# Two row scatters in flight in a fused attention and mixture-of-experts kernel

## The chip, the core and the metric

The kernel runs on one core of one Trainium2 chip. The metric is the device time of one execution in microseconds (us), the median of several runs.

## What is computed

The input is `x`, 8 sequences of 512 tokens with 256 channels (4096 tokens), in float32. One layer is computed: `x + attention(layernorm(x)) + ffn(layernorm(x))`. The attention takes a second-order Taylor series in place of the exponential. The part that matters here is the mixture of experts:

```python
logits = xf @ Wg
top_w, top_i = jax.lax.top_k(logits, TOP_K)
top_w = jax.nn.softmax(top_w, axis=-1)
one_hot = jax.nn.one_hot(top_i, E, dtype=xf.dtype)
combine = jnp.einsum('nk,nke->ne', top_w, one_hot)
h = jnp.einsum('nc,ech->enh', xf, W1)
g = jnp.einsum('nc,ech->enh', xf, W2)
y = jnp.einsum('enh,ehc->enc', jax.nn.silu(h) * g, W3)
out = jnp.einsum('enc,ne->nc', y, combine)
```

There are 8 experts (E), each token uses 2 of them (TOP_K), and an expert has 512 hidden channels. The output of a token is so the sum of its attention row and of two weighed expert rows.

## The kernel before, in words

The program is written by hand for each engine, with semaphores between the engines. It has two halves.

The first half runs over 8 batches of 512 tokens: layer norm, attention, the gate logits and the routing. GpSimd scatters each normed row twice into a scratch in HBM (`xs_scr`), sorted by expert (L467). The attention's output rows, with x added, are stored to `out` by SyncE's queue.

The second half is the mixture of experts. It runs over NT = 71 tiles of 128 sorted rows. Since each expert's rows are rounded up to whole tiles, the number of tiles in use depends on the data; 71 is the most there can be, and the rest are spare tiles, which read zero rows and add them to 128 rows behind the output. For a tile t:

- GpSimd gathers 128 rows into `xg`, four tiles ahead (`gather`, L485), and adds the 128 finished rows of the tile to `out` in HBM with an accumulating scatter (`scatter`, L496). In GpSimd's program `gather(t + 4)` stands ahead of `scatter(t)`.
- TensorE transposes the rows (L1171), multiplies with W1 and W2 (`up`, L1182), transposes the hidden rows (L1191) and multiplies with W3 (`down`, L1203). Every product is made of three, from high and low parts of float32.
- ScalarE rounds to the high parts (L619, L625), and makes the high parts of the weights of the first tiles on the way (`w12_high` L576, `w3_high` L580). VectorE makes the low parts (`expert_x` L979, `low_s` L988, `w12_low` L706, `w3_low` L711), multiplies the two hidden halves (L1009), and weighs the output rows into `yo` (`weigh_y`, L996), which has two buffers. For the first tiles TensorE waits for those low parts of the weights.
- SyncE's queue loads the weights; the last ones are issued after attention's buffers are free.

An accumulating scatter reads a row, adds and writes it. Two tiles of one expert name different tokens, but a tile of the next expert can name the same token again, and all spare tiles name the same 128 rows. Before the change each scatter waits until the one before it has landed, by one count:

```python
                    e.wait_ge(s["d_sc"], 16 * t)
```

VectorE's helper `then` lets every small instruction of the routing wait for its own semaphore before the next one starts, so these run one by one. `experts()` (L873 to L875) makes the table of each tile's expert, `texp`, which TensorE and VectorE read into a register for each tile (L1208, L991); its semaphore `v_te` also tells SyncE's queue that attention's last constants are read, so that W3 of experts 6 and 7 may be loaded over them (L396 to L398).

Of the kernel before, what the change touches and what calls it, by code (L numbers as in the profile page):

```python
# [10 lines left out]
NE = 8  # L11
HID = 512
H = 16
NT = 2 * NB + NE - 1
# [18 lines left out]
I32 = mybir.dt.int32  # L33
U32 = mybir.dt.uint32
ALU = mybir.AluOpType
# [77 lines left out]
def build(nc, x, wqk, wv, wo, w12, w3, out):  # L113
    with ExitStack() as ctx:
        s = {}
# [32 lines left out]
        minus = keep.take("minus", 4)  # L148
        A0 = room - 49152
        B0, D0, E0 = A0 + 8192, A0 + 16384, A0 + 32768  # L150
        W3h = Region(A0, B0).take("w3h", 8192, F32R, (NE * 4, D))
# [6 lines left out]

        rm = Region(344, A0)
        xg = rm.take("xg", GR * XW, F32, (GR, XW))  # L160
# [7 lines left out]

        rq = Region(344, A0)
        K2 = rq.take("K2", 2048, F32R, (2, 2, 512))  # L170
# [27 lines left out]
        def w12_lo(n):  # L198
# [76 lines left out]
                "v_rt", "v_M", "p_rk", "v_d", "a_ex", "v_slots", "v_te", "v_cw", "v_li", "p_gl", *(f"d_g{i}" for i in range(GR)), "p_gt", "a_gt", "v_gt", "v_xw", "p_h", "p_g",  # L275
                "a_si", "v_mu", "p_st", "a_st", "v_st", "p_yo", "v_yo", "d_sc")
        MISC, USED = misc_uses()
# [45 lines left out]
        def sync_program(e):  # L323
# [71 lines left out]
            done(e, "G", 0, 0)  # L395
            e.wait_ge(s["v_te"], 1)  # L396
            for n in range(6, 8):
# [4 lines left out]
            load_w12(15)  # L402
            e.wait_ge(s["d_sc"], 16 * NT)


        def gpsimd_program(e):
# [21 lines left out]
            for j in range(4):  # L428
                e.memset(below[:, j, j:4], 1.0).then_inc(s["c_below"], 1)
            e.wait_ge(s["c_iota"], 1)  # L430
            e.tensor_copy(iota[:], iota_i[:]).then_inc(s["c_const"], 1)
# [12 lines left out]
            for u in range(2):  # L444
                e.memset(xb[u][:, :, D + NE:XW], 0.0).then_inc(s["c_const"], 1)
            e.memset(zero[:], 0.0).then_inc(s["c_z"], 1)
            e.wait_ge(s["c_z"], 1)
            e.iota(zero[:, D + NE:D + NE + 1].bitcast(I32), pattern=[[0, 1]], base=NTOK, channel_multiplier=1).then_inc(s["c_z"], 1)
# [39 lines left out]
            def scatter(t):  # L488
                e.wait_ge(s["v_yo"], t + 1)
                if t == 0:  # L490
                    for b in range(4, NBATCH):
                        out_sent(e, b)
                    e.wait_ge(s["d_z"], 32)
                else:
                    e.wait_ge(s["d_sc"], 16 * t)
                e.indirect_dma_start(out, bass.IndirectOffsetOnAxis(xw[:, t % 4, NE:NE + 1].bitcast(U32), 0), yo[:, t % 2, :], None,  # L496
                                     compute_op=ALU.add).then_inc(s["d_sc"], 16)

# [157 lines left out]
        def vector_program(e):  # L656
            count = {"v_rt": 0, "v_M": 0, "v_d": 0, "v_slots": 0, "v_te": 0, "v_cw": 0, "v_li": 0,
                     "v_nt": 0}
# [214 lines left out]
            def experts():  # L873
                then(e.tensor_reduce(tf[:], cmp[:], AX.X, ALU.add))
                then(e.tensor_copy(texp[:], tf[:]), "v_te")  # L875

            e.memset(banks[:, 4, :], 0.0).then_inc(s["c_b4"], 1)
            e.wait_ge(s["c_p"], 1)
# [98 lines left out]
            def expert_x(t):  # L977
# [4 lines left out]
                if t >= 4:  # L982
                    e.wait_ge(s["d_sc"], 16 * (t - 3))
                e.tensor_copy(xw[:, t % 4, :], xg[:, t % GR, D:XW]).then_inc(s["v_xw"], 1)
# [5 lines left out]
            def weigh_y(t):  # L990
# [3 lines left out]
                if t >= 2:  # L994
                    e.wait_ge(s["d_sc"], 16 * (t - 1))
                e.tensor_scalar(yo[:, t % 2, :], banks[:, 6 + t % 2, 0:256], xw[:, t % 4, bass.ds(expert, 1)], None,  # L996
# [6 lines left out]
            for t in range(NT + 1):  # L1003
# [8 lines left out]
                if t == 0:  # L1012
                    step("o", LAST, 1)
                    w3_low(0)
                if t + 1 < NE:
                    w3_low(t + 1)
# [262 lines left out]
```

## Time and profile before

| | |
|---|---|
| median of 3 runs | 668.18 us (668.07 to 668.24) |
| span of the profiled execution | 665.4 us |
| TensorE busy | 641.8 us, 96% of the span |
| VectorE busy | 410.6 us, 62% |
| ScalarE busy | 341.6 us, 51% |
| GpSimd busy | 344.1 us, 52% |
| scatters to `out` (L496) | 71, 112.2 us busy, 154.4 us idle ahead of them |
| granted TensorE clock, mean | 0.996 |

The profile gives the span of its execution, from the first to the last instruction; no other time of that execution is recorded, and the median of the runs is 2.8 us more than the span. Busy time counts the work of an engine and not its waits for semaphores, its register loads or the issue of a DMA. What GpSimd is busy with at L485 and L496 is the making of the transfer's descriptors; the transfer itself lands later. In the names PE is TensorE, DVE VectorE, ACT ScalarE, POOL GpSimd and SP SyncE; a q behind the name is the engine's sequencer.

### The profile page before, as it was taken

How to read it: one execution, taken by the hardware profiler on the slowest of the kernel's cores; microseconds unless marked ns; L12 is line 12 of the kernel's file. 1: busy time of each engine (PE TensorE's matmuls, PEld its weight loads, DVE VectorE, ACT ScalarE, POOL GpSimd, SP SyncE). 2: the span in 40 equal slices, each digit the busy share in tenths (PEclk: the TensorE clock that was granted, in tenths of full speed). 3: DMA queues.
4: the chain of work that ended last, by engine and by line, in shares of the span. 5: the costliest groups of instructions: out<-in, count | busy, mean ns of one | idle time of the engine just before them, and what ended most of it. 6: DMA issues, size and time to landing. Idle time of an engine off the chain costs nothing.

```text
span 665.4 us, 16423 instructions
## 1 busy us (share of the span) xinstructions
PE 641.8 (96%) x5414; PEld 496.5 (75%) x5414; DVE 410.6 (62%) x1067; ACT 341.6 (51%) x515; POOL 344.1 (52%) x381
## 2 busy tenths in 40 slices
PE   8899999999999999999999999999999999999994
PEld 7555666666666666657888888888888888888883
DVE  6777788787878585777975444444544445444452
ACT  3668878787877686766642232322323223232331
POOL 3265655546463736473465555455545555455542
PEclk9999999999999999999999999999999999999998
DMA  4653555554443435447633434333333433333332
GB/s 134 141 133 99 127 153 130 152 130 147 93 136 77 128 85 154 118 150 249 207 59 58 66 51 66 50 57 60 58 59 50 66 51 57 58 51 58 58 50 25
DMA packets 37775, 64.07 MB, mean 96 GB/s; under 512 B 8289, under 2 KB 25825, under 8 KB 37697
## 3 DMA queue, kind: packets, MB, share of 16 engines
q0 software_dynamic: 16704, 28.12, 22.0%
q1 hardware_dynamic: 20432, 34.24, 20.2%
q8 instruction: 50, 0.82, 0.5%
q10 hardware_dynamic: 560, 0.66, 0.3%
q14 instruction: 29, 0.23, 0.1%
HBM read 27.72 MB, written 22.68 MB: 76 GB/s over the span
## 4 chain that ended last, share of the span: by engine, by line
PE 87%; DVE 4%; DMA 2%; ACT 2%; issue 2%; SPq 1%; ACTq 0%; POOL 0%; POOLq 0%; DVEq 0%
PE banks L1182 29%; PE banks L1203 15%; PE banks L1056 10%; PE banks L1038 8%; PE banks L1076 7%; PE banks L1191 5%; PE banks L1085 4%; PE banks L1120 3%; PE banks L1171 2%; PE banks L1105 1%; PE banks L1111 1%; DMA K<-Kt 1%; ACT T L533 1%; DVE xTl L740 1%; PE banks L1094 1%
## 5 line engine op out<-in xcount | busy, mean ns | idle before, releaser
L496 POOL DMA_INDIRECT out<-yo,xw x71 | 112.2, 1581 | 154.4 <-DVE yo L996 76.6
L625 ACT ACTIVATE sTh<-banks 128x512 fp32r<-128x512 f32 x71 | 42.5, 598 | 192.4 <-PE banks L1191 186.6
L476 POOL TENSOR_SCALAR_AFFINE_SELECT T<-T 128x512 f32<-128x512 f32 x128 | 80.8, 642 | 108.5 <-ACT T L539 43.1
L988 DVE TENSOR_TENSOR sTl<-banks,sTh 128x512 fp32r<-128x512 f32 x71 | 49.0, 691 | 118.9 <-ACT sTh L625 118.9
L1182 PE MATMUL banks<-w12h,xgh 128*128 x284 | 118.0, 415 | 0.6 <-DVE xgl L979 0.6
L1182 PE MATMUL banks<-w12l,xgh 128*128 x284 | 112.2, 395 | 0.0
L1182 PE MATMUL banks<-w12h,xgl 128*128 x284 | 112.1, 395 | 0.0
L485 POOL DMA_INDIRECT xg<-xs_scr,glist x71 | 72.4, 1020 | 21.5 <-issue 20.0
L1056 PE MATMUL banks<-T,vau 128*17 128x512 f32 (+3 forms) x1024 | 75.6, 434 | 0.9 <-POOL T L476 0.9
L467 POOL DMA_INDIRECT xs_scr<-xb,slots x64 | 64.3, 1004 | 18.7 <-issue 10.0
L1038 PE MATMUL banks<-Q,K 32*128 32x256 f32 (+2 forms) x1024 | 70.5, 358 | 3.5 <-DMA K<-Kt 2.2
L525 ACT ACTIVATE T<-banks 128x1024 f32<-128x1024 f32 x64 | 62.1, 1026 | 12.5 <-PE banks L1038 11.9
L533 ACT ACTIVATE T<-banks 128x768 f32<-128x768 f32 x64 | 48.5, 810 | 27.2 <-PE banks L1038 27.2
L1182 PEld LDWEIGHTS banks<-w12h,xgl 128*128 128x128 f32 x284 | 53.3, 188 | 12.0
L1056 PEld LDWEIGHTS banks<-T,vau 128*17 128x17 f32 x1024 | 26.0, 97 | 46.3 <-issue 38.4
L1182 PEld LDWEIGHTS banks<-w12h,xgh 128*128 128x128 f32 x284 | 53.8, 189 | 7.8 <-issue 1.0
L1038 PEld LDWEIGHTS banks<-Q,K 32*128 32x128 f32 x1024 | 38.6, 183 | 27.1 <-ACT T L525 12.7
L1182 PEld LDWEIGHTS banks<-w12l,xgh 128*128 128x128 f32 x284 | 53.9, 190 | 6.3
L996 DVE TENSOR_SCALAR yo<-banks,xw 128x256 f32<-128x256 f32 x71 | 34.3, 483 | 39.0 <-PE banks L1203 31.2
L539 ACT ACTIVATE T<-banks 128x768 f32<-128x768 f32 x64 | 48.7, 810 | 18.0 <-PE banks L1038 16.1
L1009 DVE TENSOR_TENSOR hs<-banks,hs 128x512 f32<-128x512 f32 x71 | 49.1, 692 | 10.2 <-PE banks L1182 0.9
L1203 PE MATMUL banks<-w3h,sTh 128*128 x284 | 51.1, 302 | 0.8 <-ACT sTh L625 0.8
(174 smaller groups left out, 1222.3 us busy)
## 6 DMA issues: line engine op xcount, KB each, us to landing
Q<-Q SPq DMA_DIRECT2D x128, 64.0 KB, 2.4
w12r<-w SPq DMA_DIRECT2D x16, 512.0 KB, 4.2
out<-xa SPq DMA_DIRECT2D x16, 256.0 KB
w3r<-w SPq DMA_DIRECT2D x8, 512.0 KB, 8.7
K<-Kt SPq DMA_DIRECT2D x124, 32.0 KB
xa<-x SPq DMA_DIRECT2D x7, 512.0 KB, 4.7
xg<-xs_scr,glist POOLq DMA_INDIRECT x71
out<-yo,xw POOLq DMA_INDIRECT x71
```

The source lines that it names most:

```text
L467: e.indirect_dma_start(xs_d, bass.IndirectOffsetOnAxis(slots[:, k, 4 * b + blk:4 * b + blk + 1].bitcast(U32), 0), xb[b % 2][:, blk, :], No ...
L476: e.affine_select(out=v, in_=v, pattern=[[0, 4], [1, P]], compare_op=ALU.is_ge, fill=-1.0, base=0, channel_multiplier=-1).then_inc(s["g_mk ...
L485: e.indirect_dma_start(xg[:, t % GR, :], None, xs_d, bass.IndirectOffsetOnAxis(glist[:, t:t + 1].bitcast(U32), 0)).then_inc(s[f"d_g{t % GR ...
L496: e.indirect_dma_start(out, bass.IndirectOffsetOnAxis(xw[:, t % 4, NE:NE + 1].bitcast(U32), 0), yo[:, t % 2, :], None, compute_op=ALU.add) ...
L525: e.activation(T0[n % 2][:, 2 * h:2 * h + 2, :], banks[:, 2 * h:2 * h + 2, :], ACT.Square, scale=0.25, bias=1.0).then_inc(s["a_s"], 1)
L533: e.activation(T1[:, 2 * h:2 * h + 2, :], banks[:, 2 * h:2 * h + 2, 0:384], ACT.Square, scale=0.25, bias=1.0).then_inc(s["a_s"], 1)
L988: e.tensor_tensor(sTl[:], banks[:, 5, :], sTh[:].bitcast(F32), ALU.subtract).then_inc(s["v_st"], 1)
L1009: e.tensor_tensor(hs[:], banks[:, 2 * (t % 2) + 1, :], hs[:], ALU.mult).then_inc(s["v_mu"], 1)
L1038: i = e.matmul(banks[:, r, c0:c0 + w], K2[rr, g, h, jm * P:(jm + 1) * P], Q2[g][rr, h, p, 512 - w:512], start=(p == 0), stop=(p == 1))
L1056: i = e.matmul(banks[32 * r:32 * r + HA, 4, 512 - w:512], vau[b % 2][:, jm, 4 * qd + r, :], v[:, r, :], start=(jm == 0), stop=(jm == 2), s ...
L1182: i = e.matmul(banks[:, 2 * (t % 2) + m, :], a[:, k, :], w[:, bass.ds(expert[t] * 4 + (2 * k + m), 1), :], start=(k == 0 and n == 0), stop ...
L1203: i = e.matmul(banks[:, 6 + t % 2, 0:256], a[:, k * P:(k + 1) * P], w[:, bass.ds(expert[t] * 4 + k, 1), :], start=(k == 0 and n == 0), sto ...
```

## The change

A scatter no longer waits for the one before it in every tile, but always for the one before that, on two semaphores `d_sc0` and `d_sc1` for even and odd tiles. Whether it also waits for the one just before is read from a table `held`: for scatter t the entry t - 1 is 16 * ((t - 1) // 2), plus 16 where tile t belongs to another expert than tile t - 1 or is a spare tile. GpSimd makes a constant `before` at the start, VectorE makes `held` in four instructions (`holds`) right after `w3_low(0)` in tile 0, and GpSimd reads an entry into a register before each scatter from t = 3 on. An instruction on four elements (`mark`) carries the wait for that register, and `g_hold` counts it. SyncE's loads of W3 for experts 6 and 7 wait for `v_hold` in place of `v_te`. The scratch for the descriptors of GpSimd's transfers is 8192 bytes per partition; the new tiles take some of the room.

```diff
@@ sync_program
-            e.wait_ge(s["v_te"], 1)
+            e.wait_ge(s["v_hold"], 1)
             for n in range(6, 8):
                 load_w3(n)
...
-            e.wait_ge(s["d_sc"], 16 * NT)
+            for u in range(2):
+                e.wait_ge(s[f"d_sc{u}"], 16 * ((NT + 1 - u) // 2))
@@ gpsimd_program
+            e.iota(before_i[:], pattern=[[16, 36], [0, 2]], base=0, channel_multiplier=0).then_inc(s["c_hold"], 1)
             e.wait_ge(s["c_iota"], 1)
             e.tensor_copy(iota[:], iota_i[:]).then_inc(s["c_const"], 1)
...
             e.memset(zero[:], 0.0).then_inc(s["c_z"], 1)
+            e.wait_ge(s["c_hold"], 1)
+            e.tensor_copy(before[:], before_i[:]).then_inc(s["c_hold"], 1)
@@ scatter(t)
-                else:
-                    e.wait_ge(s["d_sc"], 16 * t)
+                if t >= 3:
+                    if t == 3:
+                        e.wait_ge(s["v_hold"], 1)
+                    else:
+                        e.wait_ge(s["g_hold"], t - 3)
+                    count = 16 * ((t - 1) // 2)
+                    landed = e.value_load(held[0:1, t - 1:t], min_val=count, max_val=count + 16)
+                    e.wait_ge(s[f"d_sc{(t - 1) % 2}"], landed)
+                    e.tensor_tensor(mark[:], minus[:], minus[:], ALU.add).then_inc(s["g_hold"], 1)
+                    e.wait_ge(s[f"d_sc{t % 2}"], 16 * (t // 2))
+                elif t:
+                    e.wait_ge(s[f"d_sc{(t - 1) % 2}"], 16)
                 e.indirect_dma_start(out, bass.IndirectOffsetOnAxis(xw[:, t % 4, NE:NE + 1].bitcast(U32), 0), yo[:, t % 2, :], None,
-                                     compute_op=ALU.add).then_inc(s["d_sc"], 16)
+                                     compute_op=ALU.add).then_inc(s[f"d_sc{t % 2}"], 16)
@@ vector_program
+            def holds():
+
+                e.wait_ge(s["c_hold"], 2)
+                then(e.tensor_scalar(change[:], iota[:, 0:72], end[:, NE - 1:NE], None, ALU.is_ge))
+                then(e.tensor_tensor(part[:, 0:71], tf[:, 1:72], tf[:, 0:71], ALU.subtract))
+                then(e.tensor_tensor(change[:, 1:72], change[:, 1:72], part[:, 0:71], ALU.max))
+                then(e.scalar_tensor_tensor(held[:, 0:71], change[:, 1:72], 16.0, before[:, 0:71], ALU.mult, ALU.add), "v_hold")
...
                 if t >= 4:
-                    e.wait_ge(s["d_sc"], 16 * (t - 3))
+                    e.wait_ge(s[f"d_sc{t % 2}"], 16 * (t // 2 - 1))
...
                 if t >= 2:
-                    e.wait_ge(s["d_sc"], 16 * (t - 1))
+                    e.wait_ge(s[f"d_sc{t % 2}"], 16 * (t // 2))
...
                 if t == 0:
                     step("o", LAST, 1)
                     w3_low(0)
+                    holds()
                 if t + 1 < NE:
                     w3_low(t + 1)
@@ kernel
-    nc = bacc.Bacc("TRN2", target_bir_lowering=False, num_devices=1)
+    nc = bacc.Bacc("TRN2", target_bir_lowering=False, num_devices=1, dynamic_dma_scratch_size=8192)
```

On VectorE, at the start of the second half (the rest of tile 0 and the start of tile 1), there stood before (w3l and w12l are low parts of weights, sTl and xgl those of the hidden and of the gathered rows):

```order
L779 TENSOR_TENSOR xa_129<-banks,xa_129 128x512
L711 TENSOR_TENSOR w3l<-w3r,w3h 128x1024 x2
L706 TENSOR_TENSOR w12l<-w12r,w12h 128x1024
L988 TENSOR_TENSOR sTl<-banks,sTh 128x512
L1009 TENSOR_TENSOR hs<-banks,hs 128x512
L979 TENSOR_TENSOR xgl<-banks,xgh 128x256
```

and in the changed kernel (whose line numbers are 23 to 31 higher here):

```order
L802 TENSOR_TENSOR xa_134<-banks,xa_134 128x512
L734 TENSOR_TENSOR w3l<-w3r,w3h 128x1024
L903 TENSOR_SCALAR change<-iota,end 128x72
L904 TENSOR_TENSOR part<-tf 128x71
L905 TENSOR_TENSOR change<-change,part 128x71
L906 SCALAR_TENSOR_TENSOR held<-change,before 128x71
L734 TENSOR_TENSOR w3l<-w3r,w3h 128x1024
L729 TENSOR_TENSOR w12l<-w12r,w12h 128x1024
L1019 TENSOR_TENSOR sTl<-banks,sTh 128x512
L1040 TENSOR_TENSOR hs<-banks,hs 128x512
L1010 TENSOR_TENSOR xgl<-banks,xgh 128x256
```

Four instructions have come between the low parts of W3 of experts 0 and 1. On GpSimd, at the end of the program, there stood before (the last two gathers and the scatters of tiles 65 to 70, the last five of them in one row):

```order
L485 DMA xg<-xs_scr,glist 128x272
L496 DMA out<-yo,xw 4224x256
L485 DMA xg<-xs_scr,glist 128x272
L496 DMA out<-yo,xw 4224x256 x5
L1239 UNCONDITIONAL_BRANCH
```

and in the changed kernel (the scatters of tiles 68 to 70):

```order
L519 DMA out<-yo,xw 4224x256
L513 TENSOR_LOAD held
L513 ISA x2
L515 TENSOR_TENSOR mark<-minus 128x4
L519 DMA out<-yo,xw 4224x256
L513 TENSOR_LOAD held
L513 ISA x2
L515 TENSOR_TENSOR mark<-minus 128x4
L519 DMA out<-yo,xw 4224x256
L1271 UNCONDITIONAL_BRANCH
```

Ahead of each scatter from tile 3 on there is now a register load with two instructions of the sequencer and one small computing instruction.

## Rows read from the trace of the kernel before

**Rows 1.** busy time of each engine in three stretches (us, then instructions), granted clock, DMA

```profile
309.00:320.00 11.00, 10.25 (x62) 8.61 (x61) 9.83 (x15) 7.28 (x11) 0.00 (x0) 1.00 1.02 377
320.00:650.00 330.00, 330.00 (x2031) 287.79 (x2030) 165.27 (x349) 107.73 (x212) 175.16 (x134) 1.00 0.36 60
```

**Rows 2.** waits between 320 and 650 us: total, times, longest

```profile
POOL out L496 <- DVE yo L996: 70.2, 35, 3.3
POOL out L496 <- DMA out<-yo,xw: 47.4, 26, 3.2
...
DVE yo L996 <- DMA out<-yo,xw: 7.0, 12, 0.6
```

**Rows 3.** timeline of one steady tile, GpSimd: start, duration, instruction, idle before it

```profile
483.99 1.58 POOL L496 DMA_INDIRECT out<-yo,xw  x1 [1.99 <-DVE yo L996]
485.88 0.99 POOL L485 DMA_INDIRECT xg<-xs_scr,glist  x1 [0.30 <-issue]
```

**Rows 4.** chain that ended last, 309 to 318 us: start, duration

```profile
311.06 0.69 DVE xa L779
311.75 2.27 DVE w3l L711 x2
314.01 0.28 DVE w12l L706
...
316.35 0.34 DVE xgl L979
...
316.89 1.19 PE banks L1182 x4
```

**Rows 5.** timeline of the last tiles, weighed rows and their scatters

```profile
650.05 1.55 POOL L496 DMA_INDIRECT out<-yo,xw  x1 [3.30 <-DVE yo L996]
...
653.93 0.48 DVE L996 TENSOR_SCALAR yo<-banks,xw 128x256 f32<-128x256 f32 x1 [0.77 <-DMA out<-yo,xw]
...
654.69 1.55 POOL L496 DMA_INDIRECT out<-yo,xw  x1 [3.09 <-DVE yo L996]
...
656.90 0.48 DVE L996 TENSOR_SCALAR yo<-banks,xw 128x256 f32<-128x256 f32 x1 [1.32 <-PE banks L1203]
659.25 1.55 POOL L496 DMA_INDIRECT out<-yo,xw  x1 [3.00 <-DMA out<-yo,xw]
```

**Rows 6.** chain that ended last, one piece at its end

```profile
654.69 3.80 DMA out<-yo,xw
```

**Rows 7.** timeline of short VectorE instructions, each waiting for the one before

```profile
281.46 0.22 DVE L837 TENSOR_SCALAR rk<-end,pf 128x8 f32<-128x8 f32 x1
...
284.72 0.23 DVE L851 TENSOR_TENSOR sel<-step,rk 128x64 f32<-128x64 f32 x1
284.99 0.22 DVE L852 TENSOR_REDUCE gapt<-sel 128x8 f32<-128x64 f32 x1
...
293.00 0.34 DVE L864 SCALAR_TENSOR_TENSOR lists<-rown,gapt,dummy 128x128 f32<-128x128 f32 x1
```

**Rows 8.** VectorE's register loads: minimum, median, longest ns, then first and last start

```profile
L991 DVEq TENSOR_LOAD <-texp x71: 299/304/590, 316.8 to 654.9; - x71
...
L991 DVEq SEQ_ASSERT  x71: 23/23/35, 317.6 to 655.5; - x71
```

**Rows 9.** GpSimd's groups of small instructions: busy us, mean ns

```profile
L411 POOL TENSOR_TENSOR sm<-sm,minus 128x4 f32<-128x4 f32 x8 | 8.4, 1048 | 12.6 <-DVE sm L680 12.4
L456 POOL COPY xb<-ids_i 128x4 int32<-128x4 int32 x8 | 1.5, 192 | 0.0
```

**Rows 10.** timeline of GpSimd, a row transfer behind a computing instruction

```profile
75.14 0.98 POOL L467 DMA_INDIRECT xs_scr<-xb,slots  x1 [0.17 <-issue]
```

**Rows 11.** waits of the whole span, GpSimd for VectorE's variances

```profile
POOL sm L411 <- DVE sm L680: 12.4, 2, 9.9
```

**Rows 12.** timeline of the DMA issues of SyncE

```profile
312.27 0.92 SPq L339 DMA_DIRECT2D w3r<-w  x2
```

**Rows 13.** timeline of ScalarE, the rounding of W3 for expert 6

```profile
335.54 1.05 ACT L580 ACTIVATE w3h<-w3r 128x1024 fp32r<-128x1024 f32 x1
```

More of the change, by code:

```diff
@@ L149, in build @@
         A0 = room - 49152
+        Q1 = 4056
         B0, D0, E0 = A0 + 8192, A0 + 16384, A0 + 32768
@@ L157, in build @@
         banks = ctx.enter_context(nc.psum_tensor("banks", [P, 8, 512], F32))
-        rm = Region(344, A0)
+        rm = Region(344, Q1)
         xg = rm.take("xg", GR * XW, F32, (GR, XW))
@@ L167, in build @@
         xw = rm.take("xw", 64, F32, (4, 16))
-        rq = Region(344, A0)
+        rx = Region(Q1, A0)
+        held = rx.take("held", 72, I32)
+        mark = rx.take("mark", 4)
+        before_i = rx.take("before_i", 72, I32)
+        before = rx.take("before", 72)
+        change = rx.take("change", 72)
+        rq = Region(344, Q1)
         K2 = rq.take("K2", 2048, F32R, (2, 2, 512))
@@ L275, in build @@
                 "v_rt", "v_M", "p_rk", "v_d", "a_ex", "v_slots", "v_te", "v_cw", "v_li", "p_gl", *(f"d_g{i}" for i in range(GR)), "p_gt", "a_gt", "v_gt", "v_xw", "p_h", "p_g",
-                "a_si", "v_mu", "p_st", "a_st", "v_st", "p_yo", "v_yo", "d_sc")
+                "a_si", "v_mu", "p_st", "a_st", "v_st", "p_yo", "v_yo", "d_sc0", "d_sc1",
+                "c_hold", "v_hold", "g_hold")
         MISC, USED = misc_uses()
@@ L656, in vector_program @@
         def vector_program(e):
-            count = {"v_rt": 0, "v_M": 0, "v_d": 0, "v_slots": 0, "v_te": 0, "v_cw": 0, "v_li": 0,
+            count = {"v_rt": 0, "v_M": 0, "v_d": 0, "v_slots": 0, "v_te": 0, "v_cw": 0, "v_li": 0, "v_hold": 0,
                      "v_nt": 0}
```

## Prediction

> **What bounds the kernel now.** I read first the busy time by stretches, then who waits for whom, then the chain of work that ended last at the two places where it leaves TensorE. From 320 to 650 us, the mixture of experts once its weights are ready, TensorE is busy for 330.00 of 330.00 us [rows 1]. A tile has 30 of its instructions (12 with W1 and W2, 12 with W3, 6 transposes), so 2031 of them in 330 us are 67.7 tiles, 4.87 us each. The waits that the change is about are in the same stretch: the scatter waits 47.4 us in all for the one before it, in 26 of the tiles, and VectorE's weighing of the rows waits 7.0 us for a scatter, at most 0.6 us at once [rows 2]. None of it reaches TensorE. A steady tile on GpSimd shows why: 1.58 us for the scatter, 0.30, 0.99 for the gather, then 1.99 us with nothing to do but wait for the next weighed rows [rows 3]. So where the old wait stands in most tiles, it costs nothing.
>
> At two places something else than TensorE sets the end. In the first, 309 to 320 us, TensorE stands still for 11.00 - 10.25 = 0.75 us, and VectorE is busy for 9.83 [rows 1]. The chain goes there through VectorE from 311.06 to 316.69 us: the last attention rows, two low parts of W3, one of W1 and W2, the low and the hidden rows, `xgl`, and only then TensorE's `up` of tile 2 at 316.89 [rows 4]. The second is the end: the last two scatters. Tile 69's rows are ready at 653.93 + 0.48 = 654.41, its scatter starts at 654.69 (0.28 later), and tile 70's rows have been ready since 657.38 when its scatter starts at 659.25 behind a wait for a transfer [rows 5]. The chain has that transfer as a piece of 3.80 us, from 654.69 to 658.49 [rows 6]; the last scatter starts 0.76 us after it.
>
> **The four instructions of `holds`.** They stand between the two low parts of W3, in the middle of VectorE's part of the chain, and each waits for the one before. Instructions of this kind take 0.22 us with 8 elements and a scalar from a tensor, 0.23 with 64 and 0.34 with 128 and three inputs, and the next starts 284.99 - 284.72 - 0.23 = 0.04 us after the end [rows 7]. For 71 or 72 elements I take 0.28, 0.23, 0.23 and 0.25, with 4 x 0.04: 1.15 us. Bounds: four at 0.22, 1.04 with the gaps; four at 0.34, 1.52. What is queued behind them on VectorE is all that the chain goes through, and TensorE is at that time already waiting for it, so the 1.15 us pass on in full. Afterwards TensorE has no slack in which to win them back. Term: **+1.15 us**.
>
> **The register load and the mark.** Before each scatter from tile 3 on, GpSimd's sequencer, once the weighed rows are there, loads the register, checks it, waits for the landing with `mark`, runs `mark`, and then starts the scatter. From the start of such a load on VectorE to the end of its check pass 655.5 + 0.02 - 654.9 = 0.6 us, of which the load is 0.30 (median; 0.59 the longest) [rows 8]. A GpSimd instruction on 128x4 takes 0.19 us as a copy, 1.05 as the power in `root` [rows 9]; an addition is nearer to the copy, and I take 0.2. A transfer behind a computing instruction starts 0.17 us after it [rows 10]. That makes 0.6 + 0.2 + 0.17 = 0.97 us per scatter. In the steady tiles GpSimd's 1.99 us of waiting hide it [rows 3], and 1.0 us is left; behind it are queued the gathers, which run four tiles ahead. If that cover were gone, each tile would cost up to 0.97 us, 66 us in all.
>
> At the end there is no cover. Tile 69's scatter starts 0.97 us later, and its landing too; the one before it, which started at 650.05 [rows 5] and takes 3.80 [rows 6], has landed in either kernel. For tile 70 the load is over before the landing, and what is new behind the landing is `mark` and the gap: 0.37 us. Does tile 70 still wait for tile 69? The reference's seeded inputs, routed by its own formula, give the experts 1057, 1055, 981, 1014, 1007, 1010, 1022 and 1046 rows, that is 9 + 9 + 8 + 8 + 8 + 8 + 8 + 9 = 67 tiles. Tiles 67 to 70 are spare ones, and the table asks for the wait in each. So nothing is saved there. Term: **+1.34 us**. Bounds: 0.8 + 0.3 = 1.1 with a short check; with a load of 0.59 and `mark` like the power, 0.29 + 0.6 + 1.05 + 0.17 and 1.05 + 0.17, together 3.3 us.
>
> The row says 0.30 us for a register load, and the Trainium skill ("DMA: Bandwidth & Descriptors", Latency and other measured facts) gives a floor of some 600 ns for `tensor_load`. No median here agrees with that, only the longest one does. By the page the sum would be 0.3 us more.
>
> **What costs nothing.** The two constants on GpSimd, 0.2 us each, are made while it waits for VectorE's variances, 12.4 us in two waits of which one is 9.9 [rows 11]. SyncE's loads of W3 for experts 6 and 7 were issued at 312.27 us [rows 12]; behind `holds` they come at about 314, and the first of them is needed at 335.54 [rows 13]. The wait of `yo` and `xw` for a scatter is for the same tile as before. For the smaller descriptor scratch no row shows a price: all scatters take 1.55 to 1.58 us [rows 3, 5]. I take 0, and it would show as longer scatters or gathers.
>
> **The sum.** 1.15 + 1.34 = 2.49 us on the profiled span of 665.4, so 667.9 us of span. The runs are 2.8 us above the span, and the same difference on the other side gives 668.18 + 2.49 = **670.7 us**, 0.37% slower. Two versions of this kernel can be told apart at about 0.2%, 1.3 us.
>
> **Rivals.**
> - *One of the two costs is covered.* VectorE's order could leave a hole, so that `holds` costs nothing at TensorE. For it speaks that VectorE is busy for only 9.83 of those 11.00 us [rows 1]; against it, that the chain's pieces on VectorE follow each other without a hole from 311.06 us on [rows 4]. Then 668.18 + 1.34 = 669.5 us, on the edge of what can be told. Chance 0.10.
> - *The last scatter is freed* (the side of no change). If tile 70 were not held, its scatter would start at 657.38 + 0.28 + 0.97 = 658.63 and not at 659.25, 0.62 us earlier than before, and the time would be 668.18 + 1.15 - 0.62 = 668.7 us. It turns on one number, the entry 69 of the table, so on whether all 71 tiles are in use; the count of 67 speaks against it. Chance 0.05.
> - *GpSimd becomes the bound.* Its loop would be 0.28 + 0.6 + mark + 0.17 + 1.58 + 0.30 + 0.99 us, 4.12 with a mark of 0.2. From a mark of 0.95 on it is longer than the tile's 4.87, and the power's 1.05 is beyond that [rows 9]. The gathers ahead would hide most of the lag, and the end would pay the dear marks: 668.18 + 1.15 + 3.04 = 672.4 us. Chance 0.07.
> - *The old waits did cost* (faster). If the 7.0 us for which VectorE's weighing waited [rows 2] had reached TensorE, their end would give 668.18 + 2.49 - 7.0 = 663.7 us. TensorE's full 330 us [rows 1] speak against it. Chance 0.04.
>
> The Trainium skill ("DMA: Bandwidth & Descriptors", Rules for kernel authors) advises to issue a transfer early and to wait on its semaphore late, so that its fixed cost overlaps with work. That rule would favour this last rival; the trace agrees with it only in that the wait exists, 47.4 us of it, not in that it costs time.
>
> **How the numbers follow.** The forecast has a chance of 0.74. Its own range, from the bounds, is 1.04 + 1.1 = 2.1 to 1.52 + 3.3 = 4.8 us, most of it below 4. The range given, 669.4 to 672.6 us, takes in the first rival (669.5) and the third (672.4), and leaves out the freed scatter, the faster case and the dearest end of the bounds. Faster by over 0.2%: 0.04. Within 0.2%: the freed scatter, half of the covered case and a little of the forecast, 0.12. Slower: 0.84.
>
> **What would show it.** Four instructions of 0.22 to 0.30 us between the low parts of W3, and `up` of tile 2 at about 318.0 us where it was 316.89. A TensorE without a hole from there to 655 us, with tiles of 4.87 us. GpSimd's scatters 1.2 to 1.3 us behind the weighed rows in steady tiles where they were 0.3, and no waits for a transfer in most. At the end tile 69's scatter 1.2 us behind its rows, and tile 70's 1.1 us behind the landing of 69. It would be wrong if a register load or `mark` on GpSimd has another price than on VectorE, or if TensorE waits for gathers.

## The result and the profile after

The changed kernel takes 671.8 us (median of 6 runs, 670.12 to 673.15) against 668.37 us (6 runs) before. The ratio is 1.005, with a 95% interval of 1.0034 to 1.0066, so it is slower by 0.5%. Run again beside the experiments it took 670.77 us (8 runs) against 668.61 (25 runs), a ratio of 1.0034 (1.0020 to 1.0048). The forecast was 670.7 us, in a range of 669.4 to 672.6.

The profiled run has a span of 669.8 us, 4.4 more than the one before. The parts of it are best read apart. First, VectorE's part of the chain that ended last, which answers to [rows 4] (start, duration, what):

```profile
314.10 0.69 DVE xa L802
314.79 1.13 DVE w3l L734
315.92 0.18 DVE change L903
...
316.12 0.24 DVE part L904
...
316.39 0.24 DVE change L905
...
316.66 0.24 DVE held L906
...
316.93 0.59 DVE w3l L734
...
320.58 0.24 DVE xgl L1010
...
321.07 1.65 PE banks L1214 x6
```

The four instructions of `holds` stand in the chain, 0.27 us apart, and `up` of tile 2 follows behind all that they delay. From TensorE's first `up` of tile 0 (307.95 us, 304.89 before) to that of tile 2 it now takes 13.12 us, and it took 12.00: +1.12 us.

From there on nothing is lost. Busy time by stretches (length; TensorE, weight loads, VectorE, ScalarE, GpSimd; clock, DMA share, GB/s), which answers to [rows 1]:

```profile
309.00:322.00 13.00, 11.30 (x69) 9.60 (x68) 10.94 (x20) 7.47 (x11) 0.49 (x1) 1.00 1.01 372
322.00:655.00 333.00, 332.94 (x2049) 290.27 (x2048) 167.03 (x352) 108.52 (x213) 189.23 (x200) 1.00 0.36 61
```

From `up` of tile 2 to the weighing of tile 70's rows it takes 339.90 us, and 340.01 before. GpSimd's steady tile shows what the cover hides (timeline: start, duration, what, idle before it); rows that were ready at 483.25 are scattered from 484.63 on, 1.38 us later, where it was 0.28 in the tile of [rows 3]:

```profile
483.94 0.19 POOL L515 TENSOR_TENSOR mark<-minus 128x4 f32<-128x4 f32 x1 [1.41 <-DMA out<-yo,xw]
484.63 1.58 POOL L519 DMA_INDIRECT out<-yo,xw  x1 [0.50 <-issue]
486.51 1.00 POOL L498 DMA_INDIRECT xg<-xs_scr,glist  x1 [0.30 <-issue]
488.71 0.19 POOL L515 TENSOR_TENSOR mark<-minus 128x4 f32<-128x4 f32 x1 [1.21 <-DMA out<-yo,xw]
```

The profile names a transfer as what `mark` waits for, but it comes 0.69 us behind the rows here (0.66 in the next tile), which is the time of the register load and its check (minimum, median, longest ns, first and last start):

```profile
L513 POOLq TENSOR_LOAD <-held x68: 284/288/503, 338.7 to 661.5; - x68
L513 POOLq FUSED_REGOPS  x68: 147/153/188, 339.2 to 661.8; - x68
L513 POOLq SEQ_ASSERT  x68: 18/18/32, 339.5 to 662.0; - x68
```

The tile of [rows 3] is not typical of the kernel before. Only 27 of its 71 scatters start within 0.31 us of their rows, and 25 start more than 1.4 us behind them, nearly all because the one before has yet to land. The largest is tile 6, whose rows were ready at 347.03 and whose scatter comes 3.38 us later (timeline of the kernel before):

```profile
346.55 0.48 DVE L996 TENSOR_SCALAR yo<-banks,xw 128x256 f32<-128x256 f32 x1 [0.56 <-PE banks L1203]
...
350.41 1.58 POOL L496 DMA_INDIRECT out<-yo,xw  x1 [1.76 <-PE banks L1171]
```

The profile names a transposition of TensorE, but a scatter waits for its rows and for the landing alone, and the rows were long ready. Scatters that wait for a landing follow each other mostly 4.5 to 4.8 us apart, hardly less than a tile's 4.87, so a delay is worked off over many tiles. In the changed kernel 63 of the 71 scatters start 1.30 to 1.38 us behind their rows. So the change did what it was made for, and it brought no time, since TensorE is busy throughout in either kernel.

The last tiles, a timeline that answers to [rows 5], of VectorE's weighed rows of tiles 69 and 70 and of GpSimd:

```profile
658.02 0.48 DVE L1027 TENSOR_SCALAR yo<-banks,xw 128x256 f32<-128x256 f32 x1 [0.77 <-PE banks L1235]
...
659.16 0.19 POOL L515 TENSOR_TENSOR mark<-minus 128x4 f32<-128x4 f32 x1 [2.45 <-DMA out<-yo,xw]
...
659.81 1.55 POOL L519 DMA_INDIRECT out<-yo,xw  x1 [0.46 <-POOL mark L515]
...
660.97 0.48 DVE L1027 TENSOR_SCALAR yo<-banks,xw 128x256 f32<-128x256 f32 x1 [1.30 <-PE banks L1235]
663.66 0.19 POOL L515 TENSOR_TENSOR mark<-minus 128x4 f32<-128x4 f32 x1 [2.29 <-DMA out<-yo,xw]
664.00 1.55 POOL L519 DMA_INDIRECT out<-yo,xw  x1
```

Tile 69's scatter comes 1.31 us behind its rows (658.50) and not 0.28, +1.03 us. Tile 70's comes 4.19 us behind it and not 4.56, which is 0.37 us less, where 0.37 us more was forecast. And the span ends 5.80 us behind the last scatter's start, against 6.15. These parts and the 0.11 us less in the middle add up to +1.12 - 0.11 + 1.03 - 0.37 - 0.35 = +1.32 us, where the time from the first `up` to the end of the span has grown by 1.34.

The rest of the 4.4 us lies at the very start. The granted clock of TensorE falls to 0.50, its lower level (1.2 GHz), between 22 and 30 us (the same columns as above), where it stayed at 1.00 in the profiled run before:

```profile
20.00:24.00 4.00, 2.09 (x46) 1.18 (x46) 2.79 (x13) 2.04 (x3) 0.90 (x1) 0.87 0.49 86
24.00:28.00 4.00, 4.00 (x17) 2.53 (x17) 1.68 (x9) 1.67 (x5) 1.27 (x2) 0.50 0.92 272
28.00:32.00 4.00, 4.00 (x39) 2.77 (x43) 2.81 (x7) 3.44 (x5) 1.23 (x2) 0.77 0.27 74
```

The first `up` came 3.06 us later. Of that 0.61 us are there before the clock falls: the first weights were ready at 8.21 us and not 7.60, and TensorE restarts at 21.19 us and not 20.58. This is not the change's doing: in the twelve other profiles, those of the kernel before with nothing but an edit at its last scatter among them (`e4_mark_last`, `e8_swap`), the first weights are ready at 8.05 to 8.41 us. Another 2.33 us come from the restart to the first of VectorE's 32 `yw` instructions, one for each step of attention (12.96 us and not 10.63), while the clock is low. The profile before is of a quick execution besides: all runs with a recorded span are 1.7 to 1.8 us longer than it, and by that (an estimate) the one with 665.4 us took some 667.2, 1 us under the median. Between the fifth `yw` and the last the two kernels take the same, 236.17 us in the changed kernel and 236.01 before.

### The profile page after: what moved, and what is told of

It reads as the page before. It is cut to its first block, busy times and chain, and to the rows that moved or that the text cites. A ratio compares the mean times of both kernels' runs of the same rounds, so it can differ in the third digit from the quotient of the medians.

```text
span 669.8 us, 16703 instructions
## 1 busy us (share of the span) xinstructions
PE 645.4 (96%) x5414; PEld 498.9 (74%) x5414; DVE 410.8 (61%) x1071; ACT 341.1 (51%) x515; POOL 358.0 (53%) x451
## 4 chain that ended last, share of the span: by engine, by line
PE 90%; ACT 3%; DVE 2%; issue 2%; DMA 2%; POOL 0%; ACTq 0%; SPq 0%; POOLq 0%; DVEq 0%
PE banks L1214 29%; PE banks L1235 15%; PE banks L1088 11%; PE banks L1070 9%; PE banks L1108 7%; PE banks L1223 5%; PE banks L1152 4%; PE banks L1117 4%; PE banks L1203 2%; PE banks L1137 1%; PE banks L1143 1%; ACT T L556 1%; DMA wqk_r<-wqk 1%; DVE xTl L763 1%; PE banks L1126 1%
## 5 line engine op out<-in xcount | busy, mean ns | idle before, releaser
L498 POOL DMA_INDIRECT xg<-xs_scr,glist x71 | 73.7, 1038 | 21.5 <-issue 20.9
L1070 PE MATMUL banks<-Q,K 32*128 32x256 f32 (+2 forms) x1024 | 71.9, 363 | 3.4 <-DMA K<-Kt 1.5
L515 POOL TENSOR_TENSOR mark<-minus 128x4 f32<-128x4 f32 x68 | 13.1, 193 | 89.4 <-DMA out<-yo,xw 84.4
L1027 DVE TENSOR_SCALAR yo<-banks,xw 128x256 f32<-128x256 f32 x71 | 34.3, 483 | 42.3 <-PE banks L1235 42.3
```

What stands on the lines that cost most here:

```text
L498: e.indirect_dma_start(xg[:, t % GR, :], None, xs_d, bass.IndirectOffsetOnAxis(glist[:, t:t + 1].bitcast(U32), 0)).then_inc(s[f"d_g{t % GR ...
L1070: i = e.matmul(banks[:, r, c0:c0 + w], K2[rr, g, h, jm * P:(jm + 1) * P], Q2[g][rr, h, p, 512 - w:512], start=(p == 0), stop=(p == 1))
```

## The experiments

Since the clock falls in part of the executions of every kernel here, the times are read with the clock of each run, and the second half (from the first `up` to the end of the span) from the profiles. It is 360.51 us before and 361.85 after. Single profiles spread: `e1_scratch` and `e5_consts` have the same program there and give 360.11 and 359.52 us. So a difference of some 0.6 us in a second half is read from its parts and not from the sum. "The clock fell" stands for a mean granted clock of the run under 0.9945.

**The small scratch alone** (`e1_scratch`), the kernel before with

```diff
-    nc = bacc.Bacc("TRN2", target_bir_lowering=False, num_devices=1)
+    nc = bacc.Bacc("TRN2", target_bir_lowering=False, num_devices=1, dynamic_dma_scratch_size=8192)
```

> The kernel before with one edit: the scratch for GpSimd's descriptors is 8192 bytes, as in the changed kernel, which also moves every tile in SBUF down. It is to tell where the 3.1 us come from that the changed kernel's profiled run had lost before its first expert tile (307.95 us against 304.89), with a granted clock of 0.50 to 0.87 from 20 to 32 us. Theory A (the dip of the clock at the start comes and goes by itself, and no edit makes it): within 0.2% of before, a clock of 0.99 or more in most runs, scatters of 1.55 to 1.58 us. Theory B (the smaller scratch, or the moved tiles, slow the first loads and so bring the dip): 1.5 to 3 us slower, with the dip in the profile and a lower clock in most runs.

Measured: 667.67 us against 668.44, ratio 0.9989 (0.9971 to 1.0007), the same or a little less. The clock fell in 5 of 12 runs, so the scratch does not bring it. Between the last scatter's start and the end of the span lie 5.84 us.

**`holds` moved** (`e2_holds_early`), the changed kernel with

```diff
             step("t", LAST, 3)
+            holds()
...
                     w3_low(0)
-                    holds()
```

> The changed kernel with the four instructions of holds moved to the end of the first half, behind the last normalise and ahead of expert_x of tile 0, where VectorE had a hole of 0.72 us. Theory A (holds costs 1.15 us because it stands in VectorE's part of the chain): between the first up and the up of tile 2 it takes 12.0 us again and not 13.1; in its new place about 0.4 us stick out of the hole, so the time is 0.7 to 0.8 us below the changed kernel, some 1 to 1.5 us above before where the clock at the start is the same. Rival (the price is the later loads of W3 or another wait, not these instructions): 13.1 us stay.

Measured: 669.64 us against 668.44, ratio 1.0025 (1.0007 to 1.0042). Between the `up` of tile 0 and that of tile 2 it takes 11.99 us again. In the new place the low rows `xgl` of tile 0 now wait for them (306.52 us, right behind `held`), and TensorE's first `up` comes 0.34 us later behind the last `yw` (4.16 us and not 3.82). VectorE's timeline there:

```profile
305.05 0.42 DVE L756 TENSOR_TENSOR yn<-banks,rd 128x256 f32<-128x256 f32 x1
305.39 0.25 DVE L903 TENSOR_SCALAR change<-iota,end 128x72 f32<-128x72 f32 x1
...
306.20 0.28 DVE L906 SCALAR_TENSOR_TENSOR held<-change,before 128x71 int32<-128x71 f32 x1
306.52 0.42 DVE L1011 TENSOR_TENSOR xgl<-banks,xgh 128x256 fp32r<-128x256 f32 x1
```

So the 1.12 us are those of the place; 0.8 of them come back by moving four instructions. The rival falls.

**Constant waits in the last two tiles** (`e3_tail_const`), the changed kernel with

```diff
+                if t >= NT - 2:
+                    e.wait_ge(s[f"d_sc{(t - 1) % 2}"], 16 * ((t + 1) // 2))
+                    e.wait_ge(s[f"d_sc{t % 2}"], 16 * (t // 2))
-                if t >= 3:
+                elif t >= 3:
```

> The changed kernel with constant waits for the landing of the scatter before in tiles 69 and 70, without register load and mark there. The changed kernel's tail had +1.03 us between tile 69's rows and its scatter, but tile 70's scatter came 4.19 us after tile 69's and not 4.56. Theory A (the load and mark cost about 1.0 us at tile 69, and a wait at the head of an indirect transfer costs about 0.4 us more than one carried by the mark): tile 69's scatter 0.28 us behind its rows again, tile 70's 4.56 behind that, so the second half is 0.65 us shorter than the changed kernel's. Rival (the 4.19 came from a shorter landing with two scatters in flight): 4.2 us between them here too, and the second half 1.0 us shorter.

Measured: 671.61 us against 668.44, ratio 1.0043 (1.0026 to 1.0060). Both theories missed: tile 69's scatter did not come back to 0.28 us behind its rows (660.41), but stood at 1.21 us. GpSimd's timeline of tiles 68 to 70 shows it:

```profile
656.42 0.19 POOL L518 TENSOR_TENSOR mark<-minus 128x4 f32<-128x4 f32 x1 [2.25 <-DMA out<-yo,xw]
657.07 1.55 POOL L522 DMA_INDIRECT out<-yo,xw  x1 [0.46 <-issue]
661.62 1.55 POOL L522 DMA_INDIRECT out<-yo,xw  x1 [2.99 <-DMA out<-yo,xw]
666.02 1.55 POOL L522 DMA_INDIRECT out<-yo,xw  x1 [2.86 <-issue]
```

Tile 68's scatter, still with load and mark, was 1.3 us late, and spare tiles are chained: tile 69's comes 4.55 us after it, later than its own rows. The lateness is handed down the chain, and to be rid of it the loads must go some tiles earlier (`e7_all_off` leaves them out from tile 66 on). Tile 70's scatter comes 4.40 us after tile 69's, and the second half is 361.92 us.

**A mark ahead of the last scatter** (`e4_mark_last`), the kernel before with

```diff
                     e.wait_ge(s["d_sc"], 16 * t)
+                    if t == NT - 1:
+                        e.tensor_tensor(mark[:], minus[:], minus[:], ALU.add).then_inc(s["g_hold"], 1)
```

> The kernel before with one edit: ahead of the last scatter stands the small computing instruction mark, which so carries the wait for the scatter of tile 69. Theory A (a wait carried by a small instruction is followed by the transfer 0.34 us later, one at the head of the transfer 0.7 us): the last scatter starts 4.19 us behind the one of tile 69, 0.37 us earlier than before, and the time is 0.1 to 0.4 us lower, which is within 0.2%. Rival (the gap is the landing's): 4.56 + 0.3 us, so 0.3 us later.

Measured: 668.42 us against 668.44, ratio 0.9990 (0.9975 to 1.0004). The last scatter comes 4.58 us after tile 69's: neither the 4.19 of theory A nor the 4.86 of the rival.

```profile
657.36 1.55 POOL L499 DMA_INDIRECT out<-yo,xw  x1 [3.09 <-DVE yo L999]
661.29 0.20 POOL L498 TENSOR_TENSOR mark<-minus 128x4 f32<-128x4 f32 x1 [2.38 <-DMA out<-yo,xw]
661.94 1.55 POOL L499 DMA_INDIRECT out<-yo,xw  x1 [0.45 <-issue]
```

The landing releases `mark` after 3.93 us, and the scatter starts 0.65 us behind that, as it did without a mark. In the changed kernel it was 663.66 to 664.00, 0.34 us. The difference that is left is what the sequencer could do meanwhile, which this run argues and `e8_swap` tests: there the rows' wait was over before the load, and `mark` stood alone with the landing's wait; here `mark` has two waits, of which one holds the sequencer.

**The start's constants alone** (`e5_consts`), the kernel before with the small scratch and

```diff
+            e.iota(before_i[:], pattern=[[16, 36], [0, 2]], base=0, channel_multiplier=0).then_inc(s["c_hold"], 1)
             e.wait_ge(s["c_iota"], 1)
...
+            e.wait_ge(s["c_hold"], 1)
+            e.tensor_copy(before[:], before_i[:]).then_inc(s["c_hold"], 1)
```

> The kernel before with the 8192-byte scratch and the two constants (an iota and a cast) where the changed kernel makes them on GpSimd, at the start; nothing reads them. The TensorE clock falls for some us between 22 and 32 us in a part of the executions: in 18 of 32 runs of the kernel before the mean clock was under 0.9945, in 24 of 27 runs of the changed kernel and its two variants, in 10 of 24 of the two variants of before. Theory A (the constants' place in GpSimd's start makes the fall likelier): most runs under 0.9945, median 1 to 2 us over before. Theory B (chance, or something else of the changed kernel, as its longer program): about half of the runs, within 0.2% of before.

Measured: 667.72 us against 668.28, ratio 0.9997 (0.9979 to 1.0014); 5 of 12 runs under 0.9945. The constants do not bring the fall of the clock.

**The constants made late** (`e6_consts_late`), the changed kernel with

```diff
             root(1)
+            e.iota(before_i[:], pattern=[[16, 36], [0, 2]], base=0, channel_multiplier=0).then_inc(s["c_hold"], 1)
+            e.wait_ge(s["c_hold"], 1)
+            e.tensor_copy(before[:], before_i[:]).then_inc(s["c_hold"], 1)
             for n in range(NQ):
```

(and without them at the start).

> The changed kernel with its two constants made after the second inverse root, at about 20.4 us, where GpSimd waits 3 us for the first mask. Theory A (the constants at the start make the fall of the clock likelier): half of the runs at 0.995 or more, median 1 to 1.5 us below the changed kernel. Theory B: clock and time as the changed kernel's, about 671.8 us.

Measured: 670.25 us against 668.28, ratio 1.0028 (1.0013 to 1.0043), and 9 of 12 runs under 0.9945. Its second half is the changed kernel's, 361.69 us. Beside the changed kernel's later run of 670.77 us it tells nothing new on the clock.

**All three places off** (`e7_all_off`), the changed kernel with the constants late, `holds` at the end of the first half, and

```diff
+                if t >= NT - 5:
+                    e.wait_ge(s[f"d_sc{(t - 1) % 2}"], 16 * ((t + 1) // 2))
-                if t >= 3:
+                elif t >= 3:
```

> The changed kernel with the constants made late, holds moved to the end of the first half, and constant waits for the scatter before in tiles 66 to 70, so that no register load and mark stand near the end. Two scatters are in flight in tiles 3 to 65 as before. Theory A (the three places are the whole price, and two scatters in flight bring nothing): tile 69's scatter 0.28 us behind its rows and tile 70's 4.56 us after it, second half within 0.5 us of before, time within 0.2% of before. Rival (two scatters in flight shorten something in the middle, hidden so far by the costs): 1 us or more below before. Rival (the loads and marks in the middle cost something too): 1 us or more above it.

Measured: 669.66 us against 668.28, ratio 1.0018 (1.0002 to 1.0033). The second half is 359.92 us, 0.6 under before: tile 69's scatter stands 0.29 us behind its rows and tile 70's 4.41 behind it, and the stretch in between, with two scatters allowed in flight in 63 tiles, takes 339.85 us. It took 340.01 before, and 339.87 in `e1_scratch`, which has the same scratch and one scatter in flight. So the flight of two brings nothing, and loads and marks in the middle cost nothing. The ratio is at the edge of theory A's 0.2%, more than the second half says: 0.34 us for `holds` are in the first half and 9 of 12 runs have the fallen clock, but at equal clock 0.8 us are left (all runs together, below) where the second half and the 0.34 give -0.25. That difference of 1.0 us is not explained.

**The last scatter's waits exchanged** (`e8_swap`), the kernel before with

```diff
+                if t < NT - 1:
                     e.wait_ge(s["v_yo"], t + 1)
...
                     e.wait_ge(s["d_sc"], 16 * t)
+                if t == NT - 1:
+                    e.wait_ge(s["v_yo"], t + 1)
```

> The kernel before with the two waits of the last scatter in the other order: the landing of the scatter before first, then the weighed rows. In the kernel before the wait for the landing is an instruction of its own on the sequencer, and the transfer starts 0.66 to 0.76 us after it; the other wait travels with the transfer, which starts 0.28 us after the rows. In the kernel with mark alone the release came 3.93 us after tile 69's scatter began, and the transfer 0.65 us later, mark or no mark. Theory A (preparing an indirect transfer takes the sequencer 0.65 us, which is hidden only behind a wait that travels with the transfer): if the landing's wait now travels with it, the last scatter starts 4.1 to 4.2 us after tile 69's and not 4.56, 0.4 us saved. Rival (the 0.65 us is the time of a landing's signal): 4.56 us as before.

Measured: 668.51 us against 668.28, ratio 0.9996 (0.9978 to 1.0013). The profile shows what the runs are too coarse for, first GpSimd's last two scatters, then the separate wait, which is now that for the rows (L498) and over at 660.1 us:

```profile
657.37 1.55 POOL L499 DMA_INDIRECT out<-yo,xw  x1 [3.09 <-DVE yo L999]
661.40 1.55 POOL L499 DMA_INDIRECT out<-yo,xw  x1 [2.47 <-DMA out<-yo,xw]
```

```profile
L498 POOLq EVENT_SEMAPHORE  x1: 17/17/17, 660.1 to 660.1; - x1
```

4.03 us between them and not 4.56. The profiles of all kernels fall into three groups here: 4.39 to 4.58 us in the six in which the landing's wait holds the sequencer, 4.11 to 4.27 in the five in which it stands alone on a short `mark`, and 4.03 and 4.05 with the waits exchanged (`e8_swap`, `e10_swap_scratch`). Theory A holds: the sequencer needs some 0.65 us to prepare an indirect transfer, and does it while it waits only if the wait that comes last travels with the transfer or with an instruction ahead of it.

**The changed kernel once more** (`e9_after_again`), without an edit.

> The changed kernel itself once more, beside the others on one chip, since its price before the first expert tile hangs on a clock that falls in some executions. If the second half's +1.3 us is all that the change does: medians of the runs with a mean clock of 0.995 or more lie 1.3 us over those of before. If the change also costs something in the first half: 2 us or more over them, or hardly a run at that clock.

Measured: 670.77 us against 668.61, ratio 1.0034 (1.0020 to 1.0048). The parts repeat: 13.09 us to `up` of tile 2, 1.32 and 4.27 us at the last scatters, second half 361.89 us. All 8 runs have a mean clock under 0.9945 ("hardly a run at that clock"), which is what the second answer of the expectation asked for; it shows the likelier fall, and does not show another cost of the first half.

**Exchanged waits and small scratch** (`e10_swap_scratch`), the kernel before with the edits of `e8_swap` and `e1_scratch`.

> The kernel before with the last scatter's waits in the other order and the 8192-byte scratch: the two edits that shortened the second half, by 0.5 us between the last scatters and by 0.3 us behind the last one. Theory (both are real and add up): last scatter 4.0 to 4.1 us after tile 69's, 5.7 to 5.8 us from it to the end of the span, second half about 359.6 us against 360.5; the time 0.5 to 1 us under before, at the edge of what the runs can tell. Rival (the 0.3 us is noise of one execution): 6.1 us behind the last scatter.

Measured: 668.09 us against 668.61, ratio 0.9990 (0.9975 to 1.0005). Second half 359.47 us, 4.05 us between the last scatters and 5.79 behind the last. It is the shortest second half of all kernels here (359.52 in `e5_consts`, within the spread), 1.0 us under before, but the runs do not tell its time from that of before.

**A dear mark** (`e11_dear_mark`), the changed kernel with

```diff
-                    e.tensor_tensor(mark[:], minus[:], minus[:], ALU.add).then_inc(s["g_hold"], 1)
+                    e.tensor_tensor(mark[:], two[:], minus[:], ALU.pow).then_inc(s["g_hold"], 1)
```

(`two` holds the constant 2).

> The changed kernel with mark as a power in place of an addition (1.05 us and not 0.19), as in the third rival of the prediction. GpSimd's loop from the weighed rows on is 0.66 + 1.05 + 0.15 + 1.58 + 0.30 + 0.99 = 4.73 us if the sequencer prepares the transfer meanwhile, and 5.08 us if it does not; a tile is 4.87. Theory A (it does): no wait of TensorE, and the price is 0.55 us at tile 69 and 0.9 us at tile 70, second half about 363.3 us. Rival (the loop is over 4.87): GpSimd falls behind tile by tile, VectorE's weighing waits for scatters in the later tiles, and the time grows by 5 us or more.

Measured: 673.30 us against 668.61, ratio 1.0072 (1.0055 to 1.0089), second half 364.56 us. In the middle TensorE is not held up (324.94 of 325 us busy from 325 to 650 us): the loop stays under a tile, with 0.20 us between `mark` and scatter. At the end the price is 1.3 us more than theory A gave. Tile 69's scatter comes 3.01 us behind its rows, since in the spare tiles landing, mark and gap take 5.17 us from scatter to scatter, longer than a tile's 4.87:

```profile
655.11 1.59 POOL L521 DMA_INDIRECT out<-yo,xw  x1 [0.20 <-POOL mark L517]
659.04 1.04 POOL L517 TENSOR_TENSOR mark<-two,minus 128x4 f32<-128x4 f32 x1 [2.34 <-DMA out<-yo,xw]
660.28 1.59 POOL L521 DMA_INDIRECT out<-yo,xw  x1 [0.20 <-DVE yo L1029]
664.18 1.04 POOL L517 TENSOR_TENSOR mark<-two,minus 128x4 f32<-128x4 f32 x1 [2.31 <-DMA out<-yo,xw]
665.42 1.59 POOL L521 DMA_INDIRECT out<-yo,xw  x1 [0.20 <-issue]
```

**Load and mark with one scatter in flight** (`e12_load_mark`), the kernel before with

```diff
+                    e.value_load(texp[0:1, t:t + 1], min_val=0, max_val=NE - 1)
                     e.wait_ge(s["d_sc"], 16 * t)
+                    e.tensor_tensor(mark[:], minus[:], minus[:], ALU.add).then_inc(s["g_hold"], 1)
```

for every tile from 3 on (the waits for `v_te` and `g_hold` ahead of the load are left out here).

> The kernel before with the register load (of the tile's expert) and mark ahead of each scatter from tile 3 on, mark carrying the old wait for the scatter before; no table, no holds, one scatter in flight, and the same number of instructions on GpSimd as in the changed kernel. Theory A (load and mark cost at the end alone, about +1.0 us at tile 69 and -0.4 at tile 70): second half 361.1 us against 360.5. Rival (they cost in the middle when only one scatter is in flight): more than 362 us. For the clock at the start: if the length of GpSimd's program makes the fall likelier, three quarters of the runs are under 0.9945 here too; if not, about half.

Measured: 669.72 us against 668.61, ratio 1.0012 (0.9997 to 1.0027). Second half 360.99 us, +0.48; 340.00 us in the middle, tile 69's scatter 1.32 us behind its rows, tile 70's 4.11 behind it. Theory A holds. 8 of 12 runs have the fallen clock, between the two answers.

**All runs together.** The mean clock of a run says a good part of its time. A line through all 229 runs of the three series and the first one, with one slope and a level for each kernel, gives 0.42 us for each 0.001 of clock, with 0.6 us of scatter. The levels at equal clock, against before: changed kernel +2.2 (6 runs) and +1.8 (8), dear mark +3.6, constant waits in two tiles +2.1, constants late +1.7, `holds` moved +1.3, all off +0.8, load and mark alone +0.5, mark last 0.0, exchanged waits -0.4, small scratch -0.4, scratch and constants -0.4, scratch and exchanged waits -0.8. Each level has a standard error of 0.2 to 0.3 us. The order is that of the second halves but for `holds` moved and all off, which stand higher than theirs (360.70 and 359.92 us).

## Why the prediction was right

The forecast was +2.49 us. The second half gives +1.34 in both profiles of the changed kernel (361.85 and 361.89 against 360.51), and the levels at equal clock 1.8 to 2.2. The direction and the two places are right; one term had the wrong sign (0.7 us too much), and one cost, the likelier fall of the clock at the start, was left out. The runs are 3.4 us over before in the first series and 2.2 in the second. That 670.7 us lies so near to their 671.8 and 670.77 is in part luck, for the two errors go opposite ways.

- *`holds` between the low parts of W3, +1.15 us.* It measured +1.12. With the instructions at the end of the first half it is 0 there, and 0.34 ahead of the first `up` (`e2_holds_early`).
- *Load and mark at tile 69, +0.97.* It measured +1.03: 0.66 to the mark, 0.19 for it, 0.46 behind it. The forecast took 0.28 to the load plus 0.97; the gap of 0.46 is longer than the 0.17 of [rows 10], since the sequencer prepares the transfer there.
- *Mark and gap at tile 70, +0.37.* This is the step that failed: it measured -0.37. The wait of 0.76 us ahead of the last scatter was read as the landing's, and left in place. It is mostly the sequencer's work for an indirect transfer (0.65 us), which `mark` with its one wait lets it do ahead. `e4_mark_last` (4.58 us, two waits on the mark), `e8_swap` (4.03 us, no mark at all) and `e12_load_mark` (4.11 us, one wait on the mark, one semaphore for all scatters) tell it from the mark itself and from the change of semaphores. Over all profiles the mark alone brings 0.1 to 0.5 us and not always 0.37 (the groups under `e8_swap`).
- *The spare tiles are held.* Right: tile 70 waited for tile 69 in every version.
- *The smaller scratch, 0.* It measured -0.4 us (standard error 0.2) at equal clock in `e1_scratch` and `e5_consts`, and the end of the span comes 5.7 to 5.9 us behind the last scatter's start in all ten profiles with it, against 6.06 to 6.15 in the four without. The step "no row shows a price, I take 0" missed a small gain, whose cause is not shown.
- *Steady tiles cost nothing.* Right, 339.90 us against 340.01, also with a mark of 1.05 us. The third rival put the edge at a mark of 0.95; with a load of 0.66, a gap of 0.20 and the 1.61, 0.30 and 1.01 us of scatter, gap and gather in `e11_dear_mark` it is estimated at 1.09. The 1.99 us of cover were read from one quiet tile, which does not stand for the first 30.
- *The old waits cost nothing.* Right: with two scatters in flight and every cost off (`e7_all_off`) the middle takes the same time to 0.2 us. The rival of a gain fell. It rested on a reading that was wrong: the 7.0 us that VectorE's weighing is said to wait for a scatter. Its engine stands idle for about 0.58 us before the weighing in most tiles, mostly with TensorE's `down` named; in the changed kernel all 42.3 us of it are put down to `down`, where 31.2 of 39.0 were before.
- *What was not foreseen: the clock at the start.* A mean clock under 0.9945 came in 52 of 92 runs of before, in 30 of 60 of the variants of before with a shorter change, but in 55 of 65 of the changed kernel and its variants. The median clock of the changed kernel's first six runs is 0.991, and that of before 0.994; at 0.42 us for 0.001 these 1.3 us explain why the first median was 3.4 us over before and not about 2. It is not the scratch, nor the constants' place at the start. The length of GpSimd's program was tried once, with 8 of 12, which decides nothing. Why the fall is likelier stays open. So do the 0.4 to 1.0 us by which the levels at equal clock exceed what the profiles show (second half, and the 0.34 us of a moved `holds`) in the changed kernel and in four of its variants. In `e11_dear_mark` the level is 0.4 under it, and in the variants of before it is 0 to 0.6 over it, so part of this is spread.

## What to carry to other kernels

A wait that the profile adds up to 47 us over a span is worth nothing while the engine behind it has time to spare, and what removes it must then be free everywhere: here four short instructions stood in the one place where their engine was the bound, and a register load in the tail. Look for the few microseconds where another engine than the bound one sets the end, and put nothing there. Where transfers are chained by their landings, lateness is handed down from one to the next: it shrinks only by what a tile is longer than landing plus what is ahead of the next transfer, and grows where that is longer than the tile (5.17 us against 4.87 in `e11_dear_mark`). And one steady tile does not show how much cover there is; measure the lag between rows and scatter in all of them.

## What the runs showed of the hardware

- An indirect transfer of GpSimd starts 0.65 us after a wait that holds its sequencer (`e4_mark_last`, where a mark fills part of it; 0.76 by the chain of the kernel before), 0.28 us after one that travels with it, and 0.15 us behind a small instruction that itself waited long enough. Exchanging the order of two waits, with no instruction more, brought 0.3 to 0.6 us at the last scatter (4.03 and 4.05 us between the last two, against 4.39 to 4.58).
- A register load on GpSimd takes 0.29 us (median of 68), 0.66 us from the rows to the next instruction with its check. The Trainium skill ("DMA: Bandwidth & Descriptors", Latency and other measured facts) gives a floor of some 600 ns for `tensor_load`; the instruction's own row has half of that, while the whole way from the rows to the next instruction comes near it.
- An accumulating scatter of 128 rows of 1 KB releases its waiter 3.9 us after its start on GpSimd (3.76 to 4.01 by the start of `mark` behind it in the last tiles of seven kernels, and 4.86 once, in `e12_load_mark`).
- TensorE's granted clock went to its lower level, 1.2 GHz, in ten of the fourteen profiles, for 3.4 to 6.8 us at a stretch between 22 and 33 us (in `e3_tail_const` and `e12_load_mark` also from 11 us on). TensorE had stood still for 0.86 to 1.48 us shortly before (19.71 to 21.19 us in the changed kernel). In the four others it kept 2.4 GHz after standstills of 1.24 to 1.58 us (19.94 to 21.52 us in `e7_all_off`), so the length of this standstill alone does not decide it. By their mean clock, runs of every kernel here had the fall.
